# The first transfers in another order, and all five engines' orders laid out for it

## The chip, the cores and the metric

The kernel runs on one core of a Trainium2 chip. The core has four engines that compute: PE (TensorE, matrix products into the eight banks of PSUM), DVE (VectorE), ACT (ScalarE, which needs a table load when it goes from one set of functions to another) and POOL (GpSimd). SP (SyncE) computes nothing here; it issues the transfers of the 16 DMA engines. Each engine works off its own instructions in the order in which they are written, and waits where a semaphore tells it to. The metric is the device time of one execution in microseconds (us), as the median of several runs.

## The reference

Eight sequences (batch) of 512 tokens of width 128 pass through the same network, each by itself. Cut to what matters here:

```python
# x: (8, 512, 128), the same for every batch
h = layernorm(x); u = rmsnorm(h, norm_w)               # "xr"
dt, B, C = split(u @ xproj_w.T)                        # 8, 16, 16 columns
dt = softplus(dt @ dt_w.T + dt_b)
for t in range(512):                                   # S6: a scan over tokens, 16 states
    state = exp(dt[t] * A) * state + (dt[t] * u[t]) * B[t]
    y[t] = state @ C[t]
# then: a gated chunk attention, an FFN with int8 weights, an attention with
# 16 heads over 512 tokens, and two layers of local attention (window 64)
# with rotary tables, each with an FFN (GELU); residuals and layernorms between
```

## The kernel before

**Tiling.** A tile is 128 partitions by 512: one batch's activations, tokens or channels on the partitions. The kernel holds four streams of 18 tiles each (tiles0 to tiles3). Batches 0 to 3 take them first, batches 4 to 7 follow, each when its stream's earlier batch is done. The four are in flight at once and fill one another's waits.

**Units.** The work of a batch is cut into some 640 named units; `network()` lists them by engine. Those of the start, with the lines of their instructions: `load` (SP, L1852) brings x; `ln_stats` (DVE, L1363 and L1366) the statistics; `ln_rstd` (ACT, L1494, L1496), `ln_shift` (DVE, L1371), `ln_apply` (ACT, L1687, four instructions) the layernorm; `mean_sq` (DVE, L1384, L1386), `rms` (ACT, L1502, L1504), `xr` (DVE, L1392) the rmsnorm; `xr_turn` (PE, L635, four 128x128) turns it, `xrT` (ACT) copies it out of PSUM. Then PE's `dt_low` (L677), `dt` (L683), `bc` (L689) and `b_turned` (L697); the softplus `sp_exp`, `sp_ln`, `sp_inverse` (ACT), `sp_1pe`, `sp_rest` (DVE); `dt_sum` (DVE, L1398, L1400, L1402), `dtu` (DVE, L1163), `dtu_turn` (PE, L635). From there on each of the 16 states of a batch takes `b_diagonal` (POOL, L1802), `dbu` (PE, L711), `da` (ACT, L1542) and `h`, the scan (DVE, L1173); each pair of states takes `hc` (DVE, L1178) and `y_sum` (PE, L729). The rows C of a pair come back from DRAM by `bc_spread` (SP, L1866), since every partition needs them; `bc_spill` (L1856) wrote them there. In the attention over 16 heads PE's `row_scores` (L868, with the masks L856) are reduced by DVE's `row_max` (L1252); `max_turn` (PE, L878) follows the last of a batch; then come `pair_scores` (L889), `exps` (ACT) and `head_values` (PE, L904).

**Units of the preparation** happen once. `fetch` (SP, L1838) brings eleven constants and weights: cst (identity and means), colp (columns: biases, scales), wts_s6, wts_chunk, wts_heads and wts_window (four slices of the weights, in the order of their first use), bcst (masks in bf16), rowp (row vectors, sent to all partitions), tab (rotary tables), pre (masks and taps) and ints (the int8 weights as int32). rowp, pre, tab and ints land in the fourth stream's tiles (tiles3), so batch 3's `load` waits until what is made of them is done. From them come `tables` (DVE, L1150; needs rowp and tab), `bias_operands` (DVE, L1101 to L1106; colp and tab), `ffw` (DVE, L1141; ints), `mix` (DVE, L1123 to L1136; pre and colp), `skip` (DVE, L1333), `decay` and `qk_scale` (DVE), `bias_split` (POOL, L1783 to L1788, six instructions; rowp), `bias_products` (PE, L655 and L656; the bias operands) with `score_bias` (DVE), and `shift_products` (PE, L665, 24 products with one column; wts_window) with `hidden_bias` and `scaled_w1` (DVE).

**What sets the order.** Nothing in the program searches for one: `ORDER` holds, for each engine, a string with three characters a unit (one for the batch, 8 standing for the preparation, two for the unit's number in `network()` or `preparation()`). `BANKS` holds the PSUM bank of every product in PE's order. `orders()` reads the strings, `places()` the banks, and `run` calls one unit after the other. Waits follow from the order: a unit waits for its inputs and, on PE, for whoever read the bank before (`take`). The tables stand for 1778 units on PE, 1290 on DVE, 1538 on ACT, 330 on POOL and 204 on SP.

## Time and profile before

| | |
|---|---|
| median of 3 runs | 1645.13 us (1643.18 to 1645.58) |
| the profiled execution | 1643.63 us, span 1641.8 us |
| mean granted clock of PE | 0.981 |
| busy: PE, DVE, ACT, POOL | 1499.9, 1259.8, 1186.2, 521.1 us |
| moved by DMA | 88.20 MB, mean 54 GB/s |

The span is the time between the first and the last instruction of the profile; 1.8 us lie around it. Busy times are the union of an engine's instructions. PE's are wide, since a product counts from its issue to its modelled end and the products overlap. The chain of work that ended last is followed back from the last instruction, each step to what released it. A line "idle before <- X" names what ended an engine's wait.

### The profile page before, as it was taken

How to read it: one execution, taken by the hardware profiler on the slowest of the kernel's cores; microseconds unless marked ns; L12 is line 12 of the kernel's file. 1: busy time of each engine (PE TensorE's matmuls, PEld its weight loads, DVE VectorE, ACT ScalarE, POOL GpSimd, SP SyncE). 2: the span in 40 equal slices, each digit the busy share in tenths (PEclk: the TensorE clock that was granted, in tenths of full speed). 3: DMA queues.
4: the chain of work that ended last, by engine and by line, in shares of the span. 5: the costliest groups of instructions: out<-in, count | busy, mean ns of one | idle time of the engine just before them, and what ended most of it. 6: DMA issues, size and time to landing. Idle time of an engine off the chain costs nothing.

```text
span 1641.8 us, 35130 instructions
## 1 busy us (share of the span) xinstructions
PE 1499.9 (91%) x14164; PEld 952.0 (58%) x14164; DVE 1259.8 (77%) x2393; ACT 1186.2 (72%) x2411; POOL 521.1 (32%) x414
## 2 busy tenths in 40 slices
PE   4899999798999999999999999988898999999997
PEld 2566665344456666666666666644444566666664
DVE  4898978866568868787688989787675787778874
ACT  4657486356898978778875776844668987787886
POOL 2643400000135535544234532000012354345530
PEclk9999999799999999999999999989999999999999
DMA  5422215430001011101132411355000011001011
GB/s 189 155 102 70 91 37 110 111 63 4 7 8 28 21 24 24 24 14 40 35 105 92 129 60 58 84 121 115 5 1 14 5 40 27 18 8 27 21 34 29
DMA packets 53585, 88.20 MB, mean 54 GB/s; under 512 B 5840, under 2 KB 27088, under 8 KB 51664
## 3 DMA queue, kind: packets, MB, share of 16 engines
q1 hardware_dynamic: 53424, 85.96, 19.7%
q8 instruction: 113, 1.85, 0.5%
q14 instruction: 48, 0.39, 0.1%
HBM read 55.65 MB, written 15.60 MB: 43 GB/s over the span
## 4 chain that ended last, share of the span: by engine, by line
PE 37%; DVE 33%; ACT 21%; issue 5%; DMA 2%; SPq 1%; POOL 1%; DVEq 0%; ACTq 0%; POOLq 0%
DVE neg_max L1252 8%; ACT tiles L1645 5%; PE psum L635 4%; DVE tiles L1173 4%; PE psum L729 3%; ACT tiles L1593 3%; PE psum L936 3%; PE psum L711 3%; ACT tiles L1687 2%; PE psum L904 2%; DVE ssq L1287 2%; DVE lsum L1304 2%; PE psum L1002 2%; DVE tiles L1427 2%; DVE tiles L1178 2%
## 5 line engine op out<-in xcount | busy, mean ns | idle before, releaser
L635 PE MATMUL psum<-cst,tiles 128*128 128x128 f32 x1440 | 211.1, 282 | 28.2 <-ACT tiles L1687 3.9
L1802 POOL TENSOR_TENSOR tiles<-cst,b_columns 128x512 f32<-128x512 f32 x128 | 159.0, 1259 | 220.1 <-PE psum L711 173.9
L635 PEld LDWEIGHTS psum<-cst,tiles 128*128 128x128 f32 x1440 | 159.9, 142 | 108.8 <-issue 48.5
L1252 DVE TENSOR_REDUCE neg_max<-psum 128x2 f32<-128x1024 f32 (+3 forms) x176 | 187.4, 1120 | 44.4 <-PE psum L856 44.3
L1813 POOL TENSOR_TENSOR tiles<-tiles 128x512 f32<-128x512 f32 x64 | 81.7, 1277 | 427.7 <-DVE tiles L1428 423.3
L1645 ACT ACTIVATE tiles<-psum,lmax,invn 128x128 f32<-128x128 f32 x512 | 191.1, 480 | 23.3 <-DVE lmax L1300 14.6
L1825 POOL TENSOR_TENSOR tiles<-tiles,lsum 128x1024 f32<-128x1024 f32 x64 | 121.3, 1898 | 206.0 <-DVE lsum L1306 205.9
L1173 DVE TENSOR_TENSOR_SCAN tiles<-tiles,psum 128x512 f32<-128x512 f32 x128 | 149.3, 1203 | 18.7 <-PE psum L711 16.4
L1542 ACT ACTIVATE tiles<-tiles,colp 128x512 f32<-128x512 f32 x128 | 89.4, 717 | 87.5 <-DVE tiles L1173 80.1
L1593 ACT ACTIVATE tiles<-psum 128x1024 f32<-128x1024 f32 (+1 forms) x128 | 113.8, 922 | 44.6 <-PE psum L856 33.0
L711 PEld LDWEIGHTS psum<-tiles 128*128 128x128 f32 x1024 | 124.8, 192 | 35.0 <-issue 22.7
L711 PE MATMUL psum<-tiles 128*128 128x128 f32 x1024 | 131.9, 279 | 5.2 <-DVE tiles L1173 3.7
L856 PE MATMUL psum<-bcst 64*128 64x128 bf16 x2048 | 134.9, 223 | 0.0
L936 PE MATMUL psum<-wts,tiles 128*128 128x512 f32 x256 | 131.3, 616 | 3.0 <-DVE tiles L1428 1.2
L729 PE MATMUL psum<-tiles,cst 128*128 128x512 f32 x256 | 123.4, 609 | 7.2 <-DVE tiles L1178 7.1
L1427 DVE TENSOR_TENSOR tiles<-psum,tables 128x512 f32<-128x512 f32 x128 | 87.2, 681 | 39.7 <-ACT tiles L1737 28.6
L856 PEld LDWEIGHTS psum<-bcst 64*128 64x128 bf16 x2048 | 100.5, 99 | 28.7 <-issue 5.3
L1477 ACT ACT_TABLE_LOAD x89 | 114.2, 1283 | 2.3 <-PEq L2022 0.7
L1304 DVE TENSOR_REDUCE lsum<-tiles 128x8 f32<-128x1024 f32 x64 | 77.6, 1213 | 36.6 <-ACT tiles L1645 36.3
L1297 DVE TENSOR_REDUCE lmax<-psum 128x4 f32<-128x512 f32 x128 | 87.1, 681 | 23.5 <-PE psum L972 23.0
L868 PE MATMUL psum<-tiles 48*128 48x512 bf16 (+3 forms) x512 | 77.3, 319 | 26.8 <-DVE neg_max L1252 20.8
L904 PE MATMUL psum<-tiles 128*32 128x512 f32 (+3 forms) x1024 | 97.3, 458 | 3.5 <-ACT tiles L1593 1.8
(230 smaller groups left out, 3439.0 us busy)
## 6 DMA issues: line engine op xcount, KB each, us to landing
tiles<-bc_scratch SPq DMA_DIRECT2D x64, 512.0 KB, 3.8
v_prev<-tiles SPq DMA_DIRECT2D x112, 128.0 KB, 2.3
split_scratch<-tiles SPq DMA_DIRECT2D x96, 128.0 KB, 2.4
tiles<-split_scratch SPq DMA_DIRECT2D x32, 384.0 KB
wts<-in_wts SPq DMA_DIRECT2D x1, 3114.0 KB, 14.5
tiles<-in_x SPq DMA_DIRECT2D x8, 256.0 KB, 3.2
out<-tiles SPq DMA_DIRECT2D x8, 256.0 KB, 2.4
tiles<-in_tab SPq DMA_DIRECT2D x1, 768.0 KB, 8.6
```

Of the source, the lines that this page charges most:

```text
L635: ins = nc.tensor.transpose(ps[:, j * 128:(j + 1) * 128], src[:, j * 128:(j + 1) * 128], ident)
L711: ins = mm(ps[:, b], T(DTU)[:, b], T(S6_B[n % 2])[:, b], start=True, stop=True)
L729: ins = mm(place("y_sum", m), ident, T(S6_H[m % 2] + a), start=False, stop=(m == STATES // 2 - 1 and a == 1))
L856: ins = mm(out, bconst("ident_sw" if swap else "ident")[r], bconst(mask + "_sw" if swap else mask)[r], start=False, stop=swap)
L904: ins = mm(ps[32 * c:32 * c + 32, jk * 128:512], values_ext()[:, jk, a:a + 32], head_probs(jk, i)[:, e, :], start=(jk == 0), stop=(jk == N ...
L936: full(mm(take("lqk_in", l, j, t, freed_by=[at("qk_sq", l, j, t), at("qk_turned", l, j, t)]), lhs, wts[:, a:a + INNER], start=True, stop=T ...
L1173: nc.vector.tensor_tensor_scan(T(t), T(S6_DA[n % 3]), ready("dbu", n), 0.0, ALU.mult, ALU.add).then_inc(sem("h"), 1)
L1252: nc.vector.tensor_reduce(nm[:, j, :, i * n:(i + 1) * n], ps.rearrange("p (e n) -> p e n", e=2)[:, :, 0:n * keys].rearrange("p e (a n) -> ...
L1593: ins = fn(head_probs(jk, i), ps[:, :, 0:w], ACT.Exp)
L1645: ins = fn(pr[:, g * 128:(g + 1) * 128], ps[:, g * 128:(g + 1) * 128], ACT.Exp, bias=own(lmax)[:, j % 2, 4 * e + g:4 * e + g + 1], scale=o ...
L1802: tt(blocks(T(S6_B[n % 2])), ident.unsqueeze(1).to_broadcast([P, NJ, 128]), own(b_columns)[:, :, n:n + 1].to_broadcast([P, NJ, 128]), ALU. ...
L1825: tt(pr, pr, own(lsum)[:, j % 2, :].unsqueeze(2).to_broadcast([P, LHEADS, 128]), ALU.mult).then_inc(sem("l_probs"), 1)
```

## The change

Only the tables `ORDER` and `BANKS` are other; the units, their instructions and their waits' rules are the same. SP's first fourteen issues are in another order. All engines' orders, to the end of the program, are laid out anew: on PE, DVE and ACT a unit stands on average some 5 places from where it stood (49 at most). The diff replaces the two tables; of SP's first line:

```diff
-        "10000080480780180680880080280520080380980a80b300001002003301302101201102103202004005104006203007008009105106107108109303"
+        "00080080280110020080480380780680880580980a80b300001002201202003101102103203301004302005104006007008009105106107108303109"
```

SP, from its first instruction; tiles0 to tiles2 are the x of batches 0 to 2, and of the weights 128x296 is wts_s6, 128x640 wts_chunk, 128x512 wts_heads, 128x6228 wts_window. Before:

```order
L1852 DMA tiles1<-in_x 128x4x128
L1852 DMA tiles0<-in_x 128x4x128
L1838 DMA tiles3<-in_rowp 128x1280
L1838 DMA tiles3<-in_pre 128x288
L1838 DMA colp<-in_colp 128x60
L1838 DMA tiles3<-in_tab 128x1536
L1838 DMA tiles3<-in_ints 128x1152
L1838 DMA cst<-in_cst 128x385
L1838 DMA wts<-in_wts 128x296
L1838 DMA wts<-in_wts 128x640
L1852 DMA tiles2<-in_x 128x4x128
L1838 DMA bcst<-in_bcst 128x1152
```

and now:

```order
L1852 DMA tiles0<-in_x 128x4x128
L1838 DMA cst<-in_cst 128x385
L1838 DMA wts<-in_wts 128x296
L1838 DMA colp<-in_colp 128x60
L1852 DMA tiles1<-in_x 128x4x128
L1852 DMA tiles2<-in_x 128x4x128
L1838 DMA tiles3<-in_rowp 128x1280
L1838 DMA tiles3<-in_pre 128x288
L1838 DMA bcst<-in_bcst 128x1152
L1838 DMA tiles3<-in_tab 128x1536
L1838 DMA tiles3<-in_ints 128x1152
L1838 DMA wts<-in_wts 128x640
```

Batch 0's x, cst, wts_s6 and colp stand ahead, then the x of batches 1 and 2, and rowp, pre, bcst, tab, ints behind them; wts_chunk, wts_heads and wts_window close the row in both.

DVE, from its first instruction (stats, mv, rms and shift carry the number of the stream). Before:

```order
L1363 BN_STATS stats0<-tiles0 128x6 x4
L1366 BN_AGGR mv0<-stats0 128x2 x4
L1363 BN_STATS stats2<-tiles2 128x6 x4
L1366 BN_AGGR mv2<-stats2 128x2 x4
L1363 BN_STATS stats1<-tiles1 128x6 x4
L1366 BN_AGGR mv1<-stats1 128x2 x4
L1095 TENSOR_SCALAR colp<-colp 128x1
L1096 TENSOR_SCALAR colp<-colp 128x1
L1091 TENSOR_SCALAR colp<-small 128x16
L1150 SCALAR_TENSOR_TENSOR tables<-tiles3 128x256 x8
L1333 TENSOR_SCALAR skip<-cst,colp 128x128
```

and now:

```order
L1363 BN_STATS stats0<-tiles0 128x6 x4
L1366 BN_AGGR mv0<-stats0 128x2 x4
L1095 TENSOR_SCALAR colp<-colp 128x1
L1096 TENSOR_SCALAR colp<-colp 128x1
L1333 TENSOR_SCALAR skip<-cst,colp 128x128
L1371 SCALAR_TENSOR_TENSOR shift0<-mv0,rstd0 128x4
L1384 TENSOR_TENSOR rms0<-rstd0 128x4
L1386 TENSOR_TENSOR rms0<-rms0,mv0 128x4
L1091 TENSOR_SCALAR colp<-small 128x16
L1363 BN_STATS stats1<-tiles1 128x6 x4
L1366 BN_AGGR mv1<-stats1 128x2 x4
L1363 BN_STATS stats2<-tiles2 128x6 x4
```

Batch 0's layernorm and mean square now stand ahead of the statistics of batches 1 and 2, and tables (L1150) behind those of all three; it is followed by the bias operands, ffw and then xr of batches 0 and 1. Before, xr came after score_bias, with batch 2's ahead.

PE, from behind the bias products; L665 is shift_products, L635 on tiles is a turn. Before:

```order
L665 MATMUL psum<-colp,wts 85x1
L635 MATMUL psum<-cst,tiles0 128x128 x4
L635 MATMUL psum<-cst,tiles2 128x128 x4
L635 MATMUL psum<-cst,tiles1 128x128 x4
L697 MATMUL psum<-wts,tiles0 128x16 x4
L677 MATMUL psum<-tiles0,wts 8x512
L677 MATMUL psum<-tiles1,wts 8x512
L689 MATMUL psum<-tiles0,wts 32x512
L683 MATMUL psum<-tiles1,wts 128x512
L683 MATMUL psum<-tiles0,wts 128x512
```

and now:

```order
L656 MATMUL psum<-tiles3 128x256
L635 MATMUL psum<-cst,tiles1 128x128 x4
L635 MATMUL psum<-cst,tiles0 128x128 x4
L677 MATMUL psum<-tiles1,wts 8x512
L697 MATMUL psum<-wts,tiles0 128x16 x4
L683 MATMUL psum<-tiles1,wts 128x512
L677 MATMUL psum<-tiles0,wts 8x512
L635 MATMUL psum<-cst,tiles2 128x128 x4
L689 MATMUL psum<-tiles0,wts 32x512
L683 MATMUL psum<-tiles0,wts 128x512
```

The turns stand ahead of shift_products, batch 1's first, and batch 1's dt (L683) comes fifth of the units. shift_products now stands after batch 1's bc, just ahead of the first dtu_turn.

Further on: in DVE's order batch 2's dt_sum now stands ahead of the first scan, with scaled_w1 and batch 3's xr, and hidden_bias behind the first four scans. Between batch 0's second hc and its last stand one hc of batch 1 and batch 2's dtu; before, there stood dt_sum of batch 2 and three scans and two hc of batch 1. Batch 0's max_turn is unit 235 of PE's order instead of 226. ACT's order holds 81 table loads instead of 89: 25 instead of 29 in the first pass of the S6 and gated stages, 24 instead of 28 in the second.

## Rows read from the trace of the kernel before

**Rows 1.** The profile's page, head: span, engines' busy times, shares of the chain.

```profile
span 1641.8 us, 35130 instructions
...
PE 1499.9 (91%) x14164; PEld 952.0 (58%) x14164; DVE 1259.8 (77%) x2393; ACT 1186.2 (72%) x2411; POOL 521.1 (32%) x414
...
PE 37%; DVE 33%; ACT 21%; issue 5%; DMA 2%; SPq 1%; POOL 1%; DVEq 0%; ACTq 0%; POOLq 0%
```

**Rows 2.** Chain that ended last, first 120 us: start us, us, what.

```profile
10.30 14.50 DMA wts<-in_wts
...
24.93 4.69 PE psum L665 x24
...
30.50 2.89 PE psum L635 x12
...
34.91 3.37 PE psum L677 x4
```

**Rows 3.** Busy time by stretch: start:end, length, engines, granted clock, DMA share, GB/s.

```profile
60.00:120.00 60.00, 56.53 (x282) 37.58 (x281) 54.61 (x49) 27.42 (x39) 32.48 (x26) 0.97 0.44 145
...
300.00:360.00 60.00, 51.20 (x627) 25.19 (x627) 42.78 (x63) 32.64 (x49) 0.33 (x2) 0.82 0.45 98
```

**Rows 4.** Timeline, 0 to 31 us: start, us, engine, line, idle before and its releaser.

```profile
3.27 0.43 SPq L1838 DMA_DIRECT2D tiles<-in_tab  x1
...
4.68 0.87 DVE L1363 BATCH_NORM_STATS2 stats<-tiles 128x6 f32<-128x128 f32 x4 [4.68 <-DMA tiles<-in_x]
...
8.99 0.95 POOL L1783 MEMSET bias_parts<- 128x1024 bf16 x1 [4.64 <-DMA tiles<-in_rowp]
9.89 0.21 ACT L1483 ACTIVATE small<-colp 128x16 f32<-128x16 f32 x1 [7.87 <-DMA colp<-in_colp]
...
14.92 2.11 POOL L1788 TENSOR_TENSOR tiles<-tiles 1x1024 bf16<-1x1024 f32 x1
16.02 0.87 DVE L1363 BATCH_NORM_STATS2 stats<-tiles 128x6 f32<-128x128 f32 x4 [10.19 <-DMA tiles<-in_x]
...
18.30 2.77 DVE L1150 SCALAR_TENSOR_TENSOR tables<-tiles 128x256 f32<-128x256 f32 x8
...
21.18 0.35 DVE L1101 TENSOR_SCALAR tiles<-tiles,colp 128x256 f32<-128x256 f32 x1
...
22.49 0.76 DVE L1141 TENSOR_SCALAR ffw<-tiles 128x1152 f32<-128x1152 int32 x1
...
27.86 3.17 ACT L1687 ACTIVATE tiles<-tiles,shift,rstd 128x128 f32<-128x128 f32 x8
...
29.53 0.87 DVE L1392 TENSOR_SCALAR tiles<-tiles,rms 128x128 f32<-128x128 f32 x4 [0.59 <-ACT tiles L1687]
```

**Rows 5.** Timeline of the S6 stage, 50 to 103 us, DVE's instructions.

```profile
50.09 2.99 DVE L1163 TENSOR_TENSOR tiles<-tiles 128x512 f32<-128x512 f32 x2
...
55.70 5.67 DVE L1173 TENSOR_TENSOR_SCAN tiles<-tiles,psum 128x512 f32<-128x512 f32 x5 [1.17 <-PE psum L711]
...
70.48 1.62 DVE L1178 TENSOR_TENSOR tiles<-tiles 128x1024 f32<-128x1024 f32 x1 [1.61 <-DMA tiles<-bc_scratch]
...
74.26 0.66 DVE L1398 TENSOR_TENSOR tiles<-tiles 128x512 f32<-128x512 f32 x1
...
75.68 1.42 DVE L1402 TENSOR_TENSOR tiles<-tiles 128x512 f32<-128x512 f32 x1
...
102.07 0.68 DVE L1163 TENSOR_TENSOR tiles<-tiles 128x512 f32<-128x512 f32 x1
```

**Rows 6.** DMA issues, first 60 us: transfer, count, KB each, median us to landing.

```profile
tiles<-in_tab SPq DMA_DIRECT2D x1, 768.0 KB, 8.6
```

**Rows 7.** Timeline of PE in the score stage, 310 to 332 us.

```profile
310.98 1.94 PE L904 MATMUL psum<-tiles 128*32 128x512 f32 x8
...
331.37 1.13 PE L904 MATMUL psum<-tiles 128*32 128x512 f32 x8
```

**Rows 8.** The page's costliest groups: busy us, mean ns, idle before.

```profile
L1477 ACT ACT_TABLE_LOAD x89 | 114.2, 1283 | 2.3 <-PEq L2022 0.7
```

More of the change, by code:

```diff
@@ new lines @@
+        "74h74564z64r64y74j74m45a45b65165074p74q64k74l64v55555674s74o74w74g65274n55774x55855965374u74t65474y65574z74r65674k751750"
+        "74v55a55b75265765865975375475575675775875965a65b75a75b"),
+    "POOL": (
+        "80180010000100010120000300220110300500410200700600900800b00a00d00c00f00e10510410710610910810b10a10d10c30030110f10e202203"
+        "20420520620720820920b20a20d20c20f20e30230330430530630730930830b30a30d30c00g30f30e10g20g30g00h00i00k00l00j10h10i00m00n00o"
+        "10k10l10j00q00r00p20h20i10n10o00s10m20k20l20j10q10r10p20m20n20o10s30h30i20q30k30l20r20p30j00t00u20s30m30n30o00w00x30p30q"
+        "30r10t10u00v30s00z01010w10x00y10v01210y01310z11001120t20u20w20x20v11211330t01430u11120y20z30w11430x21030v21221321130z30y"
+        "31021431231331131440040140240340440540640740840940a40b40c40d40e40f50050150260150350450550660050750850950a50b50d50c60250f"
+        "50e60360460560660760860960a70070160b60c60d60e60f70370270570470770670970870a70b70c70d70e70f40g50g60g70g40h40i40k40l40j50h"
+        "50i40n40o40m50k50l50j40q40r40p60h60i50m50n60k50o40s60j60l50q50r50p70h70i60n60m60o50s60q60r70k70l70j60p70n70o70m60s40t40u"
+        "40w40x70q70r40v70p40y70s50t50u40z41050w50x50v41241350y41160t60u50z51060w60x41451151251370t70u60v51470w70x60z61060y70v612"
+        "61361170y70z710614712713711714"),
@@ new lines @@
+    "SP": (
+        "00080080280110020080480780380680880580980a80b300001002201202003101102103203301004302005104006007008009105106107108303109"
+        "20420520620720820930430530630730830900a00b00c10a10b10c20a20b30a20c00d00e30b30c10d10e20d20e30d30e00f00g10f10g00h20f00i20g"
+        "10h10i20h20i30f30g00j30h00k30i10j00l10k00m20j10l20k10m30j20l30k40000n20m30l30m50010n40140240340440520n60040630n700407408"
+        "40950150250360160260350450550650750850960470170260560660770360860970470570670770870940a40b40c50a50b50c40d40e60a60b70a60c"
+        "70b70c50d50e60d60e70d70e40f40g50f40h50g60f40i60g70f50h50i70g60h60i70h70i40j40k50j40l50k40m60j60k50l50m70j60l70k60m40n70l"
+        "70m50n60n70n"),
@@ L363 @@
[L363 to L364 removed]
+    "012010123012031012020342030120101301401010100101201102010241520124061247044516231205103521655360712703506010106121342601"
+    "201230120101010203150320360230430102101024602604012301240623204602302303030530523502303503030303570202406240724024202024"
+    "024020420461351351351351351735135023040404602401640146135610350137513151315371351013513513513513513531561724604240627101"
@@ new lines @@
+    "246240131431460141265626267257253141301037350306324052350647060507012135173563510710301561501456434012340134035673561271"
+    "476701030450313012516712456027143150475071206120234524521321623152740101701070145625376025051231202346712601205107134232"
+    "457130413506403253271240537301305370170102145071407256710270274574537013701050373063101573161031571257241574572456070301"
+    "251342362310126010261473042361201401362674342321306173603671650124501012313204502010231021020123123014301010341304110130"
@@ new lines @@
+    "101013040313430120340102012021032125653020315750123043547072013721301274030314013130153403113013011020120320104301230112"
+    "460246101012102350235075725273420513013571573146016330034160315073135130513157020240246024020420635035030350325702502402"
+    "042604240202402035203270246013024040224067604203503503570375350350630240606042601413461241246264124167124604704623704246"
+    "346343460352306240263013457410124674640234264027462046024534104102601213502364150103041025067015470145675605160102102536"
@@ L367 @@
+    "236203405674563457016340140341301640315047030560425673526532572501036706150723120467402523701201340102312030120131234012"
+    "340132134231234240671237456205131413513547012302574126417014102102130251502750260602412062130402301230523421671604102140"
+    "546142152124252672535613501576206501052352324120102301201210123010")
 class Waiting:
```

258 lines of the change are left out of this document (114 added, 144 removed).

## The prediction

> **What bounds the kernel now.** I read the page's head first: PE is busy 91% of a span of 1641.8 us, but of the chain that ended last only 37% is PE's, 33% DVE's and 21% ACT's [rows 1]. No engine alone is the bound; the chain passes from one to another, and time in which all of them wait is lost for good. Then I followed the chain in order of time [rows 2]. Its first 25 us hold no work: it runs through the issues on SP's queue and then through one transfer of 14.50 us, the last stage's weights (wts_window), for which the 24 small matmuls of shift_products wait. They hold PE until 29.6, and the first turn of batch data (xr_turn, L635) starts at 30.50. From there to the first scan of the S6 states, at 55.70, it is another 25.2 us [rows 5].
>
> The timeline tells why this chain must not be taken at its word [rows 4]. DVE does one batch's statistics at 4.68 and then sits 10.19 us idle for the third batch's x, which was issued eleventh. After it, from 16.02, DVE works off all that had piled up: statistics, tables (2.77 us), bias operands, ffw, mix; it ends batch 0's xr (L1392) only at 30.40. So PE's first turn had two late releasers, 0.8 us apart: shift_products on PE itself (29.6) and xr on DVE (30.4). Bringing one forward alone would give next to nothing. The change moves both: xr_turn goes ahead of shift_products on PE, and DVE's wait for the third x goes.
>
> From 60 us on DVE is busy 54.61 of 60 us and PE 56.53 [rows 3]; scans and products of four batches leave little slack. An earlier start of this stretch moves all that follows, because after the first transfers nothing is tied to a time of its own.
>
> **When the transfers land.** None is added or taken away. The table (tab) landed at 3.27 + 8.6 = 11.87 [rows 4, 6] and the last weights at 24.80 [rows 2]. Between them lie 5150.5 KB in eight transfers (576, 192.5, 148, 320, 256, 288, 256, 3114): 398 KB a microsecond, in order of issue. Up to and with the table 2094 KB had to pass; now it is 2978.5 KB, 884.5 more, so the table lands 2.2 us later, at 14.1, and ints at 15.5. The constants (cst) are now inside the first 448.5 KB, where 512 KB were there at 4.68 [rows 4]; colp is inside the first 626.5, at about 5.0 instead of 9.89. The third x ends at 1138.5 KB: between 6.3 (at that rate from 4.68) and 9.0 (the 1152 KB that rowp closed were there at 8.99). It was 16.02. The last weights still land at 24.8, since the bytes ahead of them are the same.
>
> **The new start, step by step.** ACT: statistics ready at 5.3, ln_rstd to 5.9, decay_exp, a table load of 1.28 for the sigmoid [rows 8], gate_sig, ln_apply of batch 0 at 1.6 (two of them take 3.17 [rows 4]) to 9.2, a table load back, two ln_rstd to 11.5, then rms and ln_apply of the other two; 0:rms, the last, ends at about 16.4. DVE: the mean squares at 12.1 and mix by 13.8, a wait for the table until 14.1, then tables 2.8 (16.9), bias operands 1.4 (18.3; 21.18 to 22.57 before), ffw 0.7 (19.0) [rows 4]. Then xr of batch 0 and of batch 1, 0.87 each, less what the two overlap.
>
> One cost is new here. POOL's bias_split (8.99 to 17.03, 8 us [rows 4]) had an idle DVE beside it; now rowp lands 626.5 KB later, at 10.6, and bias_split ends at 18.7, beside DVE's densest stretch. The rows bound the price: L1163 takes 0.68 us with POOL idle and 1.5 (two in 2.99) with POOL at work [rows 5]. Below, nothing is lost; above, DVE loses all that POOL has left after 14.1, 4.6 us. I take 2.0: only two or three of POOL's instructions are left by then, and each costs one of DVE's about 0.8.
> By the Trainium skill (SBUF — State Buffer, section "SBUF: two separate sides") VectorE and GpSimd take turns at a shared pair of ports, held for a whole instruction; the trace agrees with its 1.5 against 0.68. By that rule at its strictest the price would be the upper end, 4.6, and the forecast 2.6 us later.
>
> So xr of batch 0 ends at 21.9, batch 1's at 22.7, and PE's first turn (now batch 1's) starts at 22.8 instead of 30.50: 7.7 us. The first scan came 25.2 us after it. In the new PE order the first dt is the fifth unit from the first turn instead of the eighth: one turn (0.24 a matmul, 1.0) and two 128x512 products (0.84 each [rows 2]) come later, 2.7 us. But the second dt follows further behind, DVE does batch 0's dtu ahead of batch 1's while PE turns batch 1's first, and shift_products (4.69 [rows 2]) now lies between the last dt and dtu_turn. It fits into PE's idle time while DVE does the two dt_sum. I take 24.5, with 22.5 (the 2.7 gained in full) and 29.2 (shift_products fully in the way) as bounds. The first scan then starts at 47.3, 8.4 us earlier. By then DVE has also done batch 2's dt_sum, which before stood among the scans, from 74.26 to 77.10 [rows 5]; less the two small hidden_bias instructions that it still has to do, 0.3, that is 2.5 more. **Sum: 8.4 + 2.5 = 10.9 us.** Bounds: 2.0 and 2.0 better is 14.9; 2.6 and 4.7 worse is 3.6.
>
> **The rest of the order.** All five engines' orders are laid out anew to the end, but a unit moves only some 5 places on average. The units are the same, so the work is the same, but for one thing that can be counted: ACT's table loads go from 89 to 81, 8 x 1.283 = 10.3 us less [rows 8]. They go in the two passes of the S6 and gated stages, where DVE sets the pace, so I count them as nothing, and as up to 10 on the good side. The waits in 1500 us of re-laid work I take at zero on balance, with the rivals as bounds.
>
> **Forecast.** The profiled run took 1643.63 us, 1.8 more than its span; less 10.9 it is 1632.7. The median of the runs is 1.5 above the profiled one, so the forecast is 1645.13 - 10.9 = 1634.
>
> **Rivals.**
> (a) More than the start: the table loads and fewer waits in the re-laid part count too. For it, ACT is 21% of the chain [rows 1]; against it, the loads lie where DVE has 54.61 of 60 us [rows 3]. Another 10 us: 1624.
> (b) The start's gain is spent in the S6 stage. The new DVE order runs batch 0's eight pairs of states nearly alone: between its second product and its last stand one product of batch 1 and batch 2's dtu, where before there were three scans and two products of batch 1 and batch 2's dt_sum. If each pair shows one wait of the size of 1.17 (for PE) or 1.61 (for the C rows) [rows 5], 9 to 13 us go: 1645. Against it: in these rows such a wait stands once each in 20 us, not once a pair.
> (c) The reordering doesn't change the landing times, and the start stays as it was: 1645. The landings at 8.99, 9.89, 11.87, 16.02 and 24.80 are in order of issue, so I give it little.
> The Trainium skill (DMA: Bandwidth & Descriptors, section "Queues, rings and completion order") says that completion is not first-in first-out per issuing engine; by that rule (c) could hold, but none of the transfers above overtakes another.
> (d) Slower: PE spends more of the score stage at its low level. From 300 to 360 us the granted clock is 0.82 [rows 3]; eight value products (L904) take 1.94 us at 310.98 and 1.13 at 331.37 [rows 7]. 0.18 below full is 21.6 us at half speed, 10.8 us lost. In the new order batch 0's max_turn stands 9 units later, with more of batch 1's score products ahead of it, and PE's waits for DVE there are all re-laid. If the low time doubles in this pass and grows by half as much in the second, 16.2 us are lost against 10.9 gained: 1650.4. It decides from 14.2 us of loss on.
>
> **Chances.** Forecast 0.52, (a) 0.18, (b) 0.12, (c) 0.03, (d) 0.15. A measurement of this kernel tells about 0.2%, 3.3 us, from no change. Faster by more: forecast and (a), 0.70. Within: (b) and (c), 0.15. Slower: (d), 0.15. The range reaches from a little beyond (a) to just short of (d), 1620 to 1649; the forecast's own is 1630 to 1641.5, by the bounds of the sum.
>
> **What would show it.** Right: ACT's first ln_rstd before 7 us, the first use of the table on DVE near 14, PE's first L635 near 23, the first scan near 47, and from there the same work some 11 us earlier to the end. Wrong in the first term: L635 not before 26. Wrong in the carry: the first scan near 47, but batch 4's first turn less than 6 us earlier. For (b), waits of DVE at L1173 and L1178 right after the first scan; for (c), DVE idle at L1363 for 10 us; for (d), a granted clock below 0.82 between 290 and 350, or a mean below that of before.

## The result

The changed kernel takes 1670.29 us (median of 4 runs, 1669.57 to 1671.12) against 1645.36 us for the kernel before: ratio 1.0156, 95% interval 1.0142 to 1.0170. It is 25 us slower where 11 us faster were forecast, and outside the range. The profiled run's span is 1669.3 us. The page of the profile, head and three of its groups (busy us, mean ns, idle before):

```profile
span 1669.3 us, 35140 instructions
...
PE 1509.8 (90%) x14164; PEld 952.3 (57%) x14164; DVE 1275.9 (76%) x2393; ACT 1174.2 (70%) x2403; POOL 513.5 (31%) x414
...
PEclk9899998689999999999999999998999999999999
...
PE 33%; DVE 27%; ACT 23%; issue 13%; DMA 2%; POOL 2%; SPq 0%; DVEq 0%; ACTq 0%; POOLq 0%
...
L1252 DVE TENSOR_REDUCE neg_max<-psum 128x2 f32<-128x768 f32 (+3 forms) x176 | 188.2, 1119 | 68.0 <-PE psum L856 67.5
...
L1593 ACT ACTIVATE tiles<-psum 128x1024 f32<-128x1024 f32 (+1 forms) x128 | 114.1, 923 | 70.0 <-PE psum L856 52.7
...
L1477 ACT ACT_TABLE_LOAD x81 | 103.9, 1283 | 2.2 <-PEq L2022 0.7
```

and the first two of these groups in the kernel before:

```profile
L1252 DVE TENSOR_REDUCE neg_max<-psum 128x2 f32<-128x1024 f32 (+3 forms) x176 | 187.4, 1120 | 44.4 <-PE psum L856 44.3
...
L1593 ACT ACTIVATE tiles<-psum 128x1024 f32<-128x1024 f32 (+1 forms) x128 | 113.8, 922 | 44.6 <-PE psum L856 33.0
```

Against [rows 1] and [rows 8] no engine has more instructions, and eight table loads are gone. But DVE is busy 16.1 us longer at the same 2393: 5.5 us of it are the instructions of mix at the start (below), 7 are L1300 and L1290 in the local layers (59.9 and 26.2 us where they were 55.9 and 23.1), and 2.3 are L1188. With GpSimd idle they take what they took before; beside a GpSimd instruction they take longer, L1188 for one 1.11 instead of 0.53 us, which befalls it four of eight times and before never. How much of this reaches the total was not tested. PE's ten microseconds more go with the same 14164 matmuls and a mean granted clock of 0.972 instead of 0.981. What has grown besides is waiting: the chain has 13% of "issue" where it had 5%, and DVE and ACT wait longer for PE's score products (68.0 and 70.0 us where it was 44.4 and 44.6). Where the displacement arises can be read from the same steps in both traces (start in the changed kernel less start before, us; each line is one kind of step):

```
step                        batch 0  batch 1  batch 2  batch 3
xr                            -5.6     -6.7     -1.6    +16.0
k_split (S6 to heads done)    +7.6     -6.8    +10.4    -12.4
max_parts (scores)           +16.0    +16.3    +15.9    +14.8
exps, last of the batch      +18.1    +15.7    +13.7    +18.3
y_next, last of the pass     +30.7    +28.1    +29.7    +28.4
```

By the end of the first stages the start's gain of 6 us is no longer one: two batches stand 8 to 10 us late and two 7 to 12 us early. The first score stage costs all four some 16 us, the first local stages another 13, and from then on most steps stand 21 to 34 us later, to the end (batch 4's xrT 28 us).

**The start.** Timeline of DVE in the changed kernel (start, us, line, idle before and its releaser):

```profile
3.62 0.87 DVE L1363 BATCH_NORM_STATS2 stats<-tiles 128x6 f32<-128x128 f32 x4 [3.62 <-DMA tiles<-in_x]
...
12.20 4.33 DVE L1129 SCALAR_TENSOR_TENSOR small<-tiles,colp,small 128x8 f32<-128x8 f32 x3
16.56 2.16 DVE L1132 TENSOR_SCALAR small<-small 128x8 f32<-128x8 f32 x1
...
19.23 2.76 DVE L1150 SCALAR_TENSOR_TENSOR tables<-tiles 128x256 f32<-128x256 f32 x8
...
23.90 1.64 DVE L1392 TENSOR_SCALAR tiles<-tiles,rms 128x128 f32<-128x128 f32 x8
```

The long wait for a transfer is gone as forecast, but four instructions of mix, on 128x8 elements, take 6.5 us. POOL's timeline of the same stretch shows what goes on beside them, and the chain names DVE's pieces one by one (start, us, what):

```profile
12.20 1.03 POOL L1785 CAST bias_parts<-tiles 1x1024 bf16<-1x1024 f32 x1
13.30 2.11 POOL L1786 TENSOR_TENSOR tiles<-tiles,bias_parts 1x1024 f32<-1x1024 f32 x1
15.48 1.03 POOL L1787 CAST tiles<-tiles 1x1024 bf16<-1x1024 f32 x1
16.58 2.11 POOL L1788 TENSOR_TENSOR tiles<-tiles 1x1024 bf16<-1x1024 f32 x1
```

```profile
12.20 1.06 DVE small L1129
13.28 2.17 DVE small L1129
15.48 1.06 DVE small L1129
16.56 2.17 DVE small L1132
```

Each DVE instruction is as long as the POOL instruction beside it. PE's timeline, changed kernel:

```profile
25.69 1.94 PE L635 MATMUL psum<-cst,tiles 128*128 128x128 f32 x8 [0.68 <-DVE tiles L1392]
27.60 1.86 PE L677 MATMUL psum<-tiles,wts 128*8 128x512 f32 x2
...
39.10 1.02 PE L677 MATMUL psum<-tiles,wts 128*8 128x512 f32 x2
```

The first turn is at 25.69 (30.50 before [rows 2]). Then PE works at half pace to 38 us (1.86 for what later takes 1.02), and from 40 to 60 us the granted clock is low. First the kernel before, then the changed one (stretch, length, busy PE, PEld, DVE, ACT, POOL, granted clock, DMA share, GB/s):

```profile
0.00:60.00 60.00, 33.92 (x152) 22.67 (x153) 33.85 (x111) 35.84 (x79) 21.23 (x23) 0.97 0.42 155
...
40.00:60.00 20.00, 18.09 (x97) 11.87 (x96) 16.34 (x20) 18.12 (x35) 9.73 (x9) 0.91 0.23 80
```

```profile
0.00:60.00 60.00, 32.91 (x121) 20.46 (x122) 40.55 (x111) 35.56 (x77) 19.18 (x21) 0.89 0.50 173
...
40.00:60.00 20.00, 16.95 (x86) 13.89 (x85) 18.15 (x27) 16.86 (x36) 7.70 (x7) 0.66 0.44 130
```

Five microseconds earlier at the first turn, PE has done 121 matmuls by 60 us instead of 152. The first scan starts at 56.99, where it stood at 55.70 [rows 5].

**Behind the S6 stage.** The last scans of batches 0 and 2 start 6.3 and 10.6 us early, those of batches 1 and 3 5.2 and 6.8 us late. Behind them both PE and DVE are held up once. PE's timeline, changed kernel:

```profile
246.16 0.89 PE L635 MATMUL psum<-cst,tiles 128*128 128x128 f32 x4 [2.53 <-ACT tiles L1687]
...
250.02 4.36 PE L803 MATMUL psum<-tiles,ffw 128*128 128x512 f32 x6
```

PE waits for ACT's layernorm, then works off the FFN's products at a granted clock of 0.50 (248 to 252 us), and DVE stands idle 7.71 us, to 256.20, for the next of them (L808). The kernel before has no wait of DVE above 2.6 us in this stretch.

**The score stage.** SP's queue at batch 0's maxima, before and then changed (max_scratch is the small transfer, tiles<-max_scratch its way back, tiles<-split_scratch restack):

```profile
302.66 0.59 SPq L1892 DMA_DIRECT2D max_scratch<-tiles  x1
304.55 0.56 SPq L1898 DMA_DIRECT2D tiles<-max_scratch  x2
305.15 1.23 SPq L1885 DMA_DIRECT2D tiles<-split_scratch  x3
```

```profile
313.91 1.52 SPq L1885 DMA_DIRECT2D tiles<-split_scratch  x3
...
316.51 0.30 SPq L1892 DMA_DIRECT2D max_scratch<-tiles  x1
326.73 0.55 SPq L1898 DMA_DIRECT2D tiles<-max_scratch  x2
```

In the changed order 0:max_spill stands behind 2:restack. The small transfer is issued 2.6 us after the restack's first and takes 10.2 us; before, with the restack behind it, 1.9. What PE waits for between 300 and 345 us, changed kernel (us in total, times, longest), and PE's busy time in two windows of it:

```profile
PE psum L889 <- DMA tiles<-max_scratch: 9.0, 1, 9.0
PE psum L868 <- DVE neg_max L1252: 5.6, 12, 0.7
```

```profile
300.00:360.00 60.00, 42.01 (x403) 18.89 (x401) 39.92 (x49) 18.06 (x26) 0.33 (x2) 0.68 0.46 96
...
315.00:330.00 15.00, 4.75 (x38) 1.78 (x40) 9.52 (x10) 0.00 (x0) 0.00 (x0) 0.50 0.75 136
```

### The profile page after: what moved, and what is told of

Same layout as the page of the kernel before. It is cut to its first block, busy times and chain, and to the rows that moved or that the text cites. A ratio compares the mean times of both kernels' runs of the same rounds, so it can differ in the third digit from the quotient of the medians.

```text
span 1669.3 us, 35140 instructions
## 1 busy us (share of the span) xinstructions
PE 1509.8 (90%) x14164; PEld 952.3 (57%) x14164; DVE 1275.9 (76%) x2393; ACT 1174.2 (70%) x2403; POOL 513.5 (31%) x414
## 4 chain that ended last, share of the span: by engine, by line
PE 33%; DVE 27%; ACT 23%; issue 13%; DMA 2%; POOL 2%; SPq 0%; DVEq 0%; ACTq 0%; POOLq 0%
ACT tiles L1645 6%; PE psum L635 4%; PE psum L711 4%; PE psum L729 4%; DVE neg_max L1252 3%; DVE tiles L1173 3%; ACT tiles L1593 2%; ACT tiles L1687 2%; DVE ssq L1287 2%; ACT L1477 2%; DVE tiles L1427 2%; PE psum L1045 2%; PE psum L936 2%; DVE tiles L1428 2%; DVE lsum L1304 2%
## 5 line engine op out<-in xcount | busy, mean ns | idle before, releaser
L635 PE MATMUL psum<-cst,tiles 128*128 128x128 f32 x1440 | 213.4, 283 | 29.9 <-ACT tiles L1687 5.3
L1252 DVE TENSOR_REDUCE neg_max<-psum 128x2 f32<-128x768 f32 (+3 forms) x176 | 188.2, 1119 | 68.0 <-PE psum L856 67.5
L1802 POOL TENSOR_TENSOR tiles<-cst,b_columns 128x512 f32<-128x512 f32 x128 | 151.7, 1200 | 241.5 <-PE psum L711 185.9
L635 PEld LDWEIGHTS psum<-cst,tiles 128*128 128x128 f32 x1440 | 161.0, 143 | 112.5 <-issue 44.1
L1645 ACT ACTIVATE tiles<-psum,lmax,invn 128x128 f32<-128x128 f32 x512 | 191.3, 480 | 27.7 <-DVE lmax L1300 15.6
L1173 DVE TENSOR_TENSOR_SCAN tiles<-tiles,psum 128x512 f32<-128x512 f32 x128 | 149.6, 1202 | 14.9 <-PE psum L711 11.4
L1542 ACT ACTIVATE tiles<-tiles,colp 128x512 f32<-128x512 f32 x128 | 88.6, 716 | 74.5 <-DVE tiles L1173 71.5
L729 PE MATMUL psum<-tiles,cst 128*128 128x512 f32 x256 | 121.7, 600 | 1.7 <-DVE tiles L1178 1.5
L904 PE MATMUL psum<-tiles 128*32 128x128 f32 (+3 forms) x1024 | 100.2, 470 | 4.7 <-ACT tiles L1593 3.2
L889 PE MATMUL psum<-tiles 51*128 51x512 bf16 (+3 forms) x512 | 77.7, 317 | 28.1 <-DMA tiles<-max_scratch 9.0
```

What stands on the lines that cost most here:

```text
L635: ins = nc.tensor.transpose(ps[:, j * 128:(j + 1) * 128], src[:, j * 128:(j + 1) * 128], ident)
L729: ins = mm(place("y_sum", m), ident, T(S6_H[m % 2] + a), start=False, stop=(m == STATES // 2 - 1 and a == 1))
L1173: nc.vector.tensor_tensor_scan(T(t), T(S6_DA[n % 3]), ready("dbu", n), 0.0, ALU.mult, ALU.add).then_inc(sem("h"), 1)
L1252: nc.vector.tensor_reduce(nm[:, j, :, i * n:(i + 1) * n], ps.rearrange("p (e n) -> p e n", e=2)[:, :, 0:n * keys].rearrange("p e (a n) -> ...
L1645: ins = fn(pr[:, g * 128:(g + 1) * 128], ps[:, g * 128:(g + 1) * 128], ACT.Exp, bias=own(lmax)[:, j % 2, 4 * e + g:4 * e + g + 1], scale=o ...
L1802: tt(blocks(T(S6_B[n % 2])), ident.unsqueeze(1).to_broadcast([P, NJ, 128]), own(b_columns)[:, :, n:n + 1].to_broadcast([P, NJ, 128]), ALU. ...
```

## The experiments

Eighteen kernels, all with the same work unless said; the kernel before was measured beside each group and took 1644.0 to 1645.5. The times are medians, the ratios are formed from all runs, so that the two can differ by some tenths of a per cent; where two intervals overlap, I call no difference shown. Units are written batch:step, 8 is the preparation.

```
run                           us       ratio to before, 95%
e1_transfers_alone            1646.4   1.0014 [1.0001, 1.0027]
e2_orders_alone               1672.3   1.0171 [1.0140, 1.0202]
e3_maxima_first               1661.7   1.0115 [1.0087, 1.0144]
e4_mix_later                  1670.9   1.0176 [1.0144, 1.0209]
f1_new_start_old_rest         1649.8   1.0044 [1.0029, 1.0059]
f2_new_s6_old_rest            1651.9   1.0054 [1.0038, 1.0069]
f3_old_s6_new_rest            1677.0   1.0210 [1.0194, 1.0225]
f4_old_pass_new_pass          1649.1   1.0035 [1.0022, 1.0048]
g1_new_from_local             1656.5   1.0072 [1.0048, 1.0095]
g2_new_to_local               1662.3   1.0107 [1.0086, 1.0127]
g3_.._maxima_first            1654.3   1.0046 [1.0023, 1.0069]
h1_start_mended               1658.3   1.0076 [1.0061, 1.0091]
k1_shift_products_first       1681.9   1.0227 [1.0211, 1.0242]
k2_warm_after                 1667.5   1.0148 [1.0122, 1.0173]
k3_warm_before                1657.5   1.0066 [1.0046, 1.0087]
k4_new_first_local            1670.5   1.0158 [1.0140, 1.0176]
m1_before_warm_short          1643.6   0.9994 [0.9980, 1.0008]
m2_after_warm_maxima_first    1660.3   1.0096 [1.0077, 1.0115]
```

### The transfers or the orders

Transfers alone, in the kernel before (and the opposite edit in the changed kernel):

```diff
-SP: 1:load 0:load rowp pre colp tab ints cst wts_s6 wts_chunk 2:load bcst wts_heads wts_window
+SP: 0:load cst wts_s6 colp 1:load 2:load rowp pre bcst tab ints wts_chunk wts_heads wts_window
```

> The kernel before, with only SP's first fifteen entries in the new order; every other order and every bank as before. If the new order of the transfers is itself what costs the 25 us (its landings meet the kernel's first reads badly), this one is slow too: 1660 to 1670. If the loss lies in the orders that were laid anew for it, this one has none of it: its DVE still takes batch 2's statistics second and the tables sixth, so it can use little of the earlier landings either: 1638 to 1648, shift_products and xr of batch 0 within 3 us of the 29.6 and 30.4 of before.

> The changed kernel, with SP's first fifteen entries in the order of before; all other orders and banks as changed. If the transfers cost the time, this gives it back: 1640 to 1650. If the re-laid orders cost it, it stays, and the start is late by what the transfers had brought: first scan product 4 to 9 us later than in the changed kernel, total 1668 to 1680.

The transfers' order is worth next to nothing either way: with the old orders 1.0014, an interval that only just leaves out 1, and with the new ones 1.0156 with it and 1.0171 without, with overlapping intervals. The loss stays where the orders are. In one point e2 came out otherwise than expected: its first turn is 2.3 us later than in the changed kernel (28.01), but its first scan is not 4 to 9 us later; it stands at 55.55, 1.4 us earlier. So the earlier landings bring the first turn forward and, in these traces, not the first scan.

### The queue position of the maxima

```diff
 SP: 2:spill_queries 3:spill_keys
+    0:max_spill 0:max_stack
     2:restack
-    0:max_spill 0:max_stack
     3:spill_queries 3:restack
```

> The changed kernel, with batch 0's max_spill and max_stack moved on SP ahead of batch 2's restack (in the changed order they stand behind it, and the small transfer lands 10.2 us after its issue, 1.9 in the kernel before). Theory A, this queue position costs the score stage its time: batch 0's stacked maxima are there near 318 instead of 326.7, the 9.0 us wait of PE at pair_scores goes, and 8 to 12 us of the 25 come back: 1658 to 1663. Theory B, PE's and DVE's re-laid order bounds the stage whatever the transfer does: 1667 to 1671, and the wait is taken over by another.

8.6 us of the 25 come back by the medians, though the two ratios' intervals just touch (1.0087 to 1.0144 and 1.0142 to 1.0170); g3 below repeats the edit more cleanly. SP's queue now reads

```profile
310.44 0.31 SPq L1892 DMA_DIRECT2D max_scratch<-tiles  x1
312.01 0.56 SPq L1898 DMA_DIRECT2D tiles<-max_scratch  x2
312.61 1.23 SPq L1885 DMA_DIRECT2D tiles<-split_scratch  x3
```

and the 9.0 us wait is gone from PE's list: 1.6 us from issue to landing, and batch 0's first exps is 13.0 us earlier, 4.4 of them brought along from a first scan at 53.86. Up to that entry the order is the changed kernel's own, and so it is in f2, g2 and g3 below, whose first scans stand at 58.84, 57.19 and 57.13: the start differs by 5 us between traces of one order. It goes with PE's pace: its products reach full pace at 31.2 us in e3 and at 37.9 in the changed kernel, and f2 has a granted clock of 0.51 from 33 to 61 us. The granted clock from 300 to 360 us rises from 0.68 to 0.74 with the wait gone.

### The price beside GpSimd

```diff
 DVE: 2:mean_sq
-     8:mix
      8:tables 8:bias_operands 8:ffw 0:xr 1:xr
+     8:mix
      8:score_bias
```

> The changed kernel, with DVE's preparation step mix moved from before tables to after xr of batch 1. Its four small instructions stand beside POOL's one-row bias_split and took 4.33 and 2.16 us in place of 0.75 and 0.23. If they are what ate the start's gain, tables start by 15, xr of batch 0 is at 22 to 23 (25.7 in the changed kernel is the first turn of it), and the scans start 3 us earlier. If the slow span belongs to whatever DVE does beside bias_split, tables are lengthened instead and the first turn stays within 1.5 us. In the total: 1664 to 1668 if the start's gain is carried, 1668 to 1672 if the later stages swallow it.

The rival holds. mix, now at 24.5, takes 0.23 to 0.25 us an instruction, and tables takes its place beside POOL:

```profile
14.09 6.96 DVE L1150 SCALAR_TENSOR_TENSOR tables<-tiles 128x256 f32<-128x256 f32 x8 [2.19 <-DMA tiles<-in_tab]
```

6.96 us instead of 2.76. The first turn is only 0.9 us earlier, and the total the same.

### Splices by time

A splice takes each engine's list up to what its own trace shows started by a moment, and the other kernel's order for all the rest.

> Spliced orders: what the changed kernel's trace shows as started before 48 us (PE 17, DVE 29, ACT 33, GpSimd 4 and SP 21 entries) in its order, everything after it in the order of the kernel before, with one bank of 1626 chosen anew. If the new start is a gain that the old rest can carry: xr of batch 0 at 24 instead of 29.5, total 1636 to 1642. If the stages behind it swallow it: 1643 to 1648. If the start itself is harmful (PE starts cold, products at half pace until 38): over 1650.

> Spliced at 255 us: the first 180 entries of PE, 195 of DVE, 178 of ACT, 68 of GpSimd and 55 of SP (preparation, S6, chunk scan, most of the feed-forward) in the changed kernel's order, the rest in the order of the kernel before; banks unchanged. Theory A, the loss sits in the re-laid score and local stages: 1640 to 1648 here. Theory B, it was laid in S6 and only shows later: 1660 to 1670.

> The mirror image: the first 255 us in the order of the kernel before, the rest in the changed one's, one bank chosen anew. Theory A: 1662 to 1672. Theory B: 1643 to 1650. If both splices are near 1657, the loss is divided between the stretches.

> The first pass (batches 0 to 3, up to 740 us of the kernel before) in the old order, the second pass in the new one. The displacements of the changed kernel's steps hardly grow in the second pass (27 to 33 us at its start, 22 to 39 at its ends), so its order should cost nothing of its own: 1643 to 1650. If the second pass's new order costs as the first's does and the equal displacement is an accident of carried gaps: 1655 or more.

Theory A comes nearer, though f2 (1651.9) and f3 (1677.0) lie 4 and 5 us above its ranges: with the old rest behind it the new order up to 255 us costs 7.8 us, the new rest behind the old one 33. f1 lies above the 1643 to 1648 for a gain that is swallowed, and f4 (1649.1) within its range, but 5.1 us above the kernel before and clear of noise. f1 shows the start's gain lost within 30 us: xr is 5.4 us early and dt_sum 6.2, but DVE waits 2.65 us for shift_products, which the new order puts late, does batch 3's xr, and the first scan is at 58.02. From there the displacement is 2.2 to 2.7 us at every step up to 850 us: under one and the same order, displacement is carried as it is. Later, between 1090 and 1150 us, it grows to 5.8; e1, whose orders are those of before on all engines but SP, grows there by the same 3 us, so traces of one order differ by that much.

Matmul groups of PE up to 260 us show one thing that the new start loses (first the kernel before, then f2; busy us, mean ns):

```profile
L683 PE MATMUL psum<-tiles,wts 8*128 8x512 f32 x8 | 4.2, 626 | 0.0
L689 PE MATMUL psum<-tiles,wts 128*32 128x512 f32 x8 | 4.2, 602 | 0.0
```

```profile
L689 PE MATMUL psum<-tiles,wts 128*32 128x512 f32 x8 | 6.8, 947 | 0.0
L683 PE MATMUL psum<-tiles,wts 8*128 8x512 f32 x8 | 6.4, 888 | 0.0
```

Most of the same matmuls run at half pace; by 60 us f2 has done 107 matmuls, the kernel before 152. But the S6 stage itself does not end late: the last scans of batches 0 and 2 start 4.5 and 9.0 us early, those of batches 1 and 3 7.0 and 8.5 us late. Behind the seam at 255 us all four stand 9 to 10 us late. Close to it lies the place shown for the changed kernel: f2 has the same 2.53 us wait of PE, at 247.85, and DVE then waits 8.96 us for PE, up to 259.15. How much of the 7.8 us is this wait, how much the start's pace and how much the seam, no run separates.

> Order of the kernel before up to 380 us (start, S6 and batch 0's score stage), the changed kernel's order from there (the rest of the score stages of batches 1 to 3, the local stages, the second pass); 11 of 1626 banks chosen anew. The displacements of the changed kernel's steps grow by 12 to 13 us between the end of the score stage and the first pass's y_next. Theory A1, the local stage's new order costs that much whatever stands ahead of it: 1654 to 1660. Theory A2, that growth belongs to the late score stage ahead of it (its steps meet another mix of work): 1643 to 1650.

> The changed kernel's order up to 396 us (start, S6, batch 0's score stage), the order of before from there; two banks chosen anew. With S6 new and the rest old the time was 1651.9. Theory A1: the score stage adds its 7 to 10 us and the local stage nothing, 1657 to 1663. Theory A2: 1664 to 1670.

> The same as the one before it, with batch 0's max_spill and max_stack ahead of batch 2's restack on SP. If that queue position is all that the new order of the score stage costs, this comes down to the 1651.9 of the splice at 255 us: 1649 to 1654. If more of that stage's order costs time, 8 to 10 us below the run before it, but above 1655.

A1 on both. From the old end the new order costs 7.8 us to 255 us (f2), 10.4 more through batch 0's score stage (g2), and the last 8 in what follows (the changed kernel against g2). Of the 10.4, the queue position is 8.0 (g3 against g2, intervals apart, with both traces at the same displacement of 16 us when batch 0's maxima are ready); the 2.4 that g3 has over f2 is not clear of noise (1.0046 and 1.0054, by the ratios even the other way). In the local stage it is PE that stands idle longer: of the 300 us from 480 to 780 its busy time is, in g2 and then g1,

```profile
480.00:780.00 300.00, 288.72 (x3196) 189.27 (x3191) 236.37 (x442) 249.69 (x572) 144.76 (x107) 1.00 0.10 21
```

```profile
480.00:780.00 300.00, 283.20 (x3076) 185.05 (x3075) 235.72 (x416) 239.85 (x552) 144.24 (x107) 1.00 0.10 21
```

288.41 in the kernel before and 282.11 in the changed one: it follows the local stage's order and not what stood ahead of it. It is spread over waits of which none is longer than 1.8 us.

> Three pieces: the order of before up to 380 us, the changed kernel's order for the rest of the first pass (to 780 us), the order of before for the second pass; the splice at 380 with all of the rest new measured 1656.5, that with only the second pass new 1649.1, before 1644.0. If the losses of the pieces add, this is 1649 to 1654; if the first local stage holds all of it and the second pass's 5 us belong to the seam, 1654 to 1658.

The pieces do not add, and 1670.5 is far outside both expectations. Up to the seam at 780 us k4 is displaced as g1 is (batch 0's y_next 15.6 and 17.0 us); at the seam batches 1 to 3 go to 26 us, where g1 has 14.5 to 16. So a seam in the dense part can cost 10 us of its own, and f1's 5.7, f2's 7.8 and f4's 5.1 us are upper ends for their pieces. The comparisons that rest on one edit (e3 with the changed kernel, g3 with g2) have no new seam.

### The start mended by hand

```diff
 DVE: 1:dt_sum 3:ln_shift 0:dt_sum
+     0:dtu 1:dtu
      3:mean_sq
-     8:scaled_w1 8:hidden_bias 3:xr
-     2:sp_1pe 0:dtu 1:dtu 2:sp_rest
+     2:sp_1pe 2:sp_rest
      0:h1 0:h0 1:h1
+     8:scaled_w1 8:hidden_bias 3:xr
```

(Shown are DVE's entries, against f1; those of PE, ACT and SP moved to match.)

> The new start with the old rest (1649.8), with its seam mended by hand: batch 0's and 1's dtu, dtu_turn, dtuT and first dbu ahead of shift_products, scaled_w1, hidden_bias and batch 3's first chain on PE, DVE and ACT; that DVE wait of 2.65 us for shift_products and the xr of batch 3 stood ahead of them. The first scan, 55.7 in the kernel before and 58.0 in the splice, should start at 50 to 53. If the gain of a start is carried by an order that otherwise stays as it was, the total is 1638 to 1643; if a later wait (batch 3's late first chain, a transfer) eats it, 1644 to 1648 although the first scan is early.

The first scan is at 53.19, near the 50 to 53 expected, and the kernel is 8.5 us slower than without the mend, outside both of the totals. ACT and then DVE in h1 (timelines):

```profile
61.79 0.69 ACT L1508 ACTIVATE tiles<-psum,colp 128x512 f32<-128x512 f32 x1 [8.24 <-PE psum L635]
...
68.46 2.33 DVE L1173 TENSOR_TENSOR_SCAN tiles<-tiles,psum 128x512 f32<-128x512 f32 x2 [9.96 <-ACT tiles L1542]
```

I had left ACT's xrT of batch 3 ahead of the next decay factors (L1542). It waited 8.24 us for a turn that now came later, and DVE 9.96 for ACT. From 68 us to the first pass's end the displacement is 9.4 to 12.9 us: one blocked in-order engine, carried to the end.

### PE's pace

k1 moves one entry of the changed kernel's PE order; k2 and k3 add idle matmuls to bias_products, in the changed kernel and in the one before:

```diff
 PE: 8:bias_products
+    8:shift_products
     1:xr_turn 0:xr_turn ... 2:dt 1:bc
-    8:shift_products
```

```diff
 def bias_products():
+    prepared("fetched", "cst")
+    warm = psum[:, bank[ONCE, "bias_products", ()], :]
+    for _ in range(32):
+        mm(warm[:, 0:384], const("ident"), cst[:, 0:384], start=True, stop=True)
     pe.wait_ge(*once("bias_operands"))
```

(These four lines shift all later line numbers by 4 in k2, k3, m1 and m2: L681 is the L677 of the others.)

> The changed kernel, with shift_products back at its old place on PE, ahead of the first turn (five banks chosen anew). In every kernel with the new start the granted clock falls to 0.50 for 12 to 28 us between 32 and 60 us (0.62 for under 4 us in the kernel before). Theory C, the fall answers PE's earlier dense work: with the 24 narrow products ahead the first turn stands at 29 to 30 as before, the low stretch is short (under 6 us at 0.5), and the first scan is at 55 to 59 all the same: total 1666 to 1672, since what the start loses the clock gives. Rival, the low stretch belongs to the new order of the engines and not to PE's early work: it stays over 10 us long, and the total is 1673 to 1680.

> The changed kernel, with 32 idle matmuls of PE (128x384, float32, from the constants into bias_products' bank, overwritten by it) ahead of its first product, in the 17 us in which PE has nothing to do. The kernel's first 128x512 products take 0.93 us each up to 31 to 38 us, later 0.51. Theory D, PE starts at half pace because it stood idle: with the warm matmuls they take 0.51 from the first, 4 to 6 us are gained at the first scan, unless theory C holds as well: then the 0.50 stretch comes earlier and is as long, and the first scan moves by under 2 us. Total 1664 to 1668 by D alone, 1668 to 1674 by both.

> The same 32 idle matmuls in the kernel before. Its first releasers are late for other reasons (weights at 24.8, xr at 29.5), so that only the products between 33 and 38 us at half pace can be gained, 3 us; by theory D 1641 to 1643, by C and D together 1643 to 1650 with a longer stretch at 0.50 than the 4 us of before.

k1 is 36.7 us slower than before, 11.6 slower than the changed kernel (1681.9, above both ranges), and theory C falls: the first turn stands at 29.02, the first scan at 67.69, and the low stretch has not shrunk:

```profile
52.00:68.00 16.00, 9.57 (x42) 6.52 (x42) 12.57 (x20) 12.91 (x28) 5.86 (x5) 0.61 0.27 89
```

PE's products stay at half pace to 54 us, with waits between them:

```profile
48.46 1.86 PE L677 MATMUL psum<-tiles,wts 128*8 128x512 f32 x2 [1.97 <-ACT tiles L1698]
```

In k2 the idle matmuls took 22.65 us, not the 17 I had allowed, and held bias_products up by 3.3 us; even so the first turns and products go at full pace. The first scan is at 54.79, 2.2 us earlier than in the changed kernel's trace, but e3 had 53.86 without idle matmuls, and the intervals of the two ratios overlap (1.0122 to 1.0173 and 1.0142 to 1.0170): no gain is shown. PE's timeline, and the window from 40 to 60 us, in which the granted clock is as low as in the changed kernel:

```profile
27.35 1.04 PE L635 MATMUL psum<-cst,tiles 128*128 128x128 f32 x8
28.79 1.02 PE L681 MATMUL psum<-tiles,wts 128*8 128x512 f32 x2 [0.40 <-ACT tiles L1512]
```

```profile
40.00:60.00 20.00, 17.79 (x85) 13.21 (x84) 19.44 (x29) 17.32 (x36) 10.21 (x9) 0.66 0.50 156
```

k3's 32 matmuls ended at 36.3 and moved everything by 13 us; it says nothing on the theories. So:

> The kernel before with 13 idle matmuls instead of 32 (one took 0.71 us, so they end near 22, before bias_operands at 22.6; the 32 ended at 36.3 and pushed everything back by 13 us). Theory D alone: the turns and 128x512 products between 30.5 and 38 go at full pace, the first scan is 2 to 4 us earlier and so is the rest, whose order is unchanged: 1640 to 1643. With theory C the low granted clock comes earlier and lasts longer and the first scan is within 1.5 us of the kernel before's: 1643 to 1646.

> The changed kernel with both mends: batch 0's maxima ahead of batch 2's restack on SP (alone 1661.7), and 26 idle matmuls that end near 23 (32 gave 1667.5 although they held bias_products up by 3.3 us). If the two add: 1655 to 1660. If they don't, because the earlier score stage meets other waits: 1660 to 1664.

m1 is no change (0.9994): its idle matmuls end at 24.3, but the granted clock is at 0.50 to 0.76 from 28 to 44 us, the four matmuls of dt_low (L681 here) still take 3.58 us at 34.18, and the first scan is at 55.97. On the order of before, warm matmuls move the low stretch, they do not save it. In the changed kernel m2 is 10.0 us below the changed kernel, and 1.4 below e3, which has the queue's mend alone; the intervals of these two overlap, so what the idle matmuls add is not shown. No version is clearly faster than the kernel before.

## Why the prediction was wrong

**The reading of before and the landings** were right. tables' data was there at 14.09 (14.1 forecast; the wait that shows it is e4's), colp at 5.79 (about 5.0), batch 2's statistics began at 7.62 (x between 6.3 and 9.0), ACT's first ln_rstd stood at 4.86 (below 7). ACT was not late either.

**The price beside POOL: placed wrongly and too small.** I laid it on tables, at 2.0 us with 4.6 as the upper end, and left out that mix, just ahead of it, ran beside four POOL instructions. It is 5.5 us on mix (4.33 and 2.16 where e4 has 0.75 and 0.23), or 4.2 on tables when mix is away (e4). The rule that I quoted and took only as an upper end, that the ports are held for a whole instruction (Trainium skill, SBUF — State Buffer, "SBUF: two separate sides"), agrees with the rows to 0.06 us: 2.17 beside 2.11. The right count was one whole POOL instruction for each of DVE's, up to POOL's end at 18.7. First turn: 25.69 instead of 22.8. I also counted this price at the start alone; of DVE's 16.1 us more, some 10 lie elsewhere.

**From the first turn to the first scan: outside its bounds.** 31.3 us, where I took 24.5 with 29.2 as the worst. I took the durations of before as they stood: there, PE had 24 narrow products behind it when the turns came, and a clock of 0.91 from 40 to 60 us. Started earlier, PE ran its first 12 us at half pace and had 0.66 after that. What the same order gave with other clocks, 27.5 in e3 (26.40 to 53.86) and 27.4 in k2, is still 3 us over my value. I read that as the place of shift_products and of batch 3's first chain; h1, which moves them behind dtu, has 27.2 where f1 has 32.1, so their place costs time, though with clocks that differ too. So the first term was -1.3 instead of 8.4. The second term, 2.5 for batch 2's dt_sum, was not measured by itself: that step came 20.9 us earlier, and no gain of it is left in the total. The check that I named for it (L635 not before 26) would hardly have caught it: L635 was at 25.69, and the time went behind it. Why the clock falls in this stretch stays open; it is not the order of the narrow products (k1) and not the idle start alone (m1).

**The carry: right where the order stays.** Behind a start whose following order is unchanged, a displacement is carried as it is: 2.2 to 2.7 us in f1, 9.4 to 12.9 in h1, some 13 in k3, to the end of the first pass. The forecast applied it to an order that had been re-laid.

**"The rest of the order at zero on balance": the step that decided.** From 255 us on it is 33 us behind the old order and 18 behind the new one, a seam included in the first. That a unit moves five places on average says nothing of the one that stands ahead of a 1.5 MB transfer. Of the 25 us, some 8 are SP's 0:max_spill behind 2:restack (e3, g3), and that cause is shown by the edit. Up to 8 are the stretch to 255 us, where the half-paced PE of the start and the wait behind ACT's layernorm are seen but were not mended one by one; the rest of the score stage is not clear of zero; and some 8 are the local stages and the second pass, in many small waits of PE that I did not resolve further. Their cause stays open.

**The rivals.** (a) fell: the eight table loads are gone, ACT is busy 12 us less, and nothing was gained. (b) named the S6 stage as the place where the start's gain goes; its sign failed: DVE's waits at L1173 and L1178 between 55 and 130 us were 5.7 us, 7.2 before, and PE's waits for DVE's products (L729 behind L1178) fell between 60 and 260 us from 4.9 to 0.7 us. (c) fell: the landings came forward, as above. (d) had the sign, its place and its check (0.68, below 0.82), but the clock was not the whole price: of the 9 us for which PE stood still, the cause was a queue, and with that mended the stage's new order costs nothing clear of noise over the old one (g3 against f2). Its bound, 16 us lost, was too small: it let one mechanism act in one kind of stage only, and the changed order lost in three places.

## What to carry to other kernels

A hand-laid order for several in-order engines is one object. When it is laid anew from a new start, count the start's gain as one term and give the re-laid remainder a range of its own size, and look in it for single entries: a small transfer that somebody waits for, behind a large one in the same queue; an instruction that blocks an in-order engine for a batch that isn't there yet. If only the start is to be gained, keep the rest of the order, though f1 and h1, which did, gained nothing here: an earlier start meets PE at another clock, and durations read later in the trace don't hold for it.

## What the runs showed of the hardware

- A VectorE instruction on 128x8 elements, 0.23 us alone, took 2.17 us beside a two-operand GpSimd instruction of 2.11 us on a single partition, and 1.06 beside a cast of 1.03. With mix away, tables was lengthened in its place (6.96 instead of 2.76 us, e4). Not every instruction was: one on 128x1 elements took 0.15 us at 11.72 beside GpSimd's of 11.69 to 12.13, and 0.14 alone (e4). In the local layers L1300, on 128x4 elements, took 0.16 us with GpSimd idle and 0.66 beside it (means in the changed kernel).
- A small transfer (max_scratch, 48 KB) landed 1.6 to 1.9 us after its issue where restack's stood behind it (e3, before), and 10.2 us when the transfers of restack, some 1.5 MB, were issued in the 2.6 us ahead of it in the same queue.
- PE's first matmuls ran at half pace, with 1.00 shown as granted: up to 31.2 us in e3 and up to 37.9 in the changed kernel, from 24.07 and 23.36, and up to 54 us where waits lay between them (k1). With idle matmuls ahead of them the first product took 1.02 us instead of 1.86 (k2).
- With PE busy 17 to 18 of 20 us, the granted clock between 40 and 60 us stood at 0.66 in the changed kernel and e3, at 0.50 in f2 and at 0.91 in the kernel before; the same order gave first scans between 53.86 and 58.84.
